# A decoder layer on one core: the middle layer on tokens sorted by matrix, in 14 pairs of tile and matrix

## Chip, cores and metric

The kernel runs on one core of a Trainium2 chip. The metric is the device time of one execution in microseconds (us).

## What is computed

The input x is 4 sequences of 256 tokens with 256 features, float32. Three layers follow each other, each added to its input and each working on the normalised input:

```python
x = x + attention(_layernorm(x), ...)          # 16 heads of 128, weights = codes * scales
x = x + xattn(_layernorm(x), tok, ctx, ctx, ctx)
x = x + moe(_layernorm(x), ...)                # 32 experts, 4 per token, and a shared one

# xattn, the middle layer: one of 4 matrices of 256 x 256 per token, by token id
expert_ids = jnp.minimum(tid // tokens_per_expert, E - 1)      # VOCAB 12500, E 4
for e in range(E):
    g = jax.nn.silu(jnp.einsum('bsd,fd->bsf', hidden_states, Wg[e]))
    u = jnp.einsum('bsd,fd->bsf', hidden_states, Wu[e])
    y = jnp.einsum('bsf,df->bsd', g * u, Wd[e])
    out = jnp.where((expert_ids == e)[..., None], y, out)
```

In this layer gate, up and down are the same matrix (ctx), so g = silu(z), u = z with one product z. In the last layer a token's 4 experts come from the router's scores, their outputs are weighted and summed.

## The kernel before

1024 tokens are 8 tiles of 128 (two halves of 4). Every float32 product of the first two layers is made of three float32r matmuls on high and low parts (mm3, L766 to L770). The operand on the moving side has 256 or 512 columns. Each engine has its own program and queue; they meet at semaphores. SyncE (SP) sends most DMAs, GpSimd (POOL) the indirect ones.

**Attention** runs in 8 groups of two heads; the last group (Plan.last) has four more slots to drain. Its last four output projection tiles are added to the residual x_acc by L1324, two token tiles at a time. The first half is normalised (ln_vector, ln_tensor, ln_high, ln_low, L689 to L759) beside this drain, the second behind it. GpSimd makes the weights' low parts (prep) and, in pieces of 128 tokens, the masks of the four matrices (masks, L606).

**Middle layer** (L892 to L934): 16 steps n of (half, matrix e, feature half ft). `pre` makes z of 512 tokens (6 matmuls of 512 columns), ScalarE takes the SiLU (L1220), GpSimd multiplies it with the mask (L656), VectorE with z (L1428), ScalarE and VectorE split it in high and low part (L1215, L1412), and `post`, three steps behind, adds four token tiles of 256 columns into the banks of the half (12 matmuls). All 8 steps of a half accumulate there, and L1418 adds them to x_acc. GpSimd also writes a piece of the table iota_s (L659) per step. The last half's normalisation goes on behind it (L1435), then router logits (L969), and the first expert weights (20 DMAs, L528 to L530) are sent by SyncE as soon as the last residual sum of attention is there (L519). Behind them in its queue stands the store of the normalised rows (L535), which the gathers read.

**Expert layer**: 64 tiles of 128 slots, in 8 trips of 8. GpSimd gathers the rows of the first 32 tiles (L667, a ring of 8). Per tile TensorE turns rows (L1056), runs gate and up (L942), turns the hidden part (L946) and runs down (L950); ScalarE takes SiLU and copies (L1235, L1240, L1292); VectorE copies and multiplies (L1555, L1561, L1442). SyncE stores each tile's output to memory (L550) and counts the stores that have landed. Trips 0 to 3 are unrolled with row work, 4 to 6 are a loop, 7 stands alone; on ScalarE and SyncE 1 to 6 and 1 to 7 are loops. VectorE does other work beside the tiles: slot tables in trips 0 to 2 (L1592 to L1623), the shared expert's sum in trip 3 (L1627), the weights of the four experts in trips 4 and 5 (L1566, L1572, L1579, L1586). From the table of slots GpSimd gathers the four outputs of every token, 32 gathers in all (L684), each after the stores that it needs; the first wait is for the table (S_NEED). When the tiles are done VectorE adds these (L1669), and SyncE stores the result.

## Time and profile before

| | us |
|---|---|
| median of 3 runs | 573.28 (571.64 to 573.55) |
| profiled execution | 574.22 |
| its span, first to last instruction | 572.3 |
| TensorE matmuls busy | 510.2 (89%) |
| VectorE, ScalarE, GpSimd busy | 424.0, 289.0, 201.8 |
| mean granted TensorE clock | 0.956 |

Times in rows are microseconds from the start of the span unless marked ns. PE is TensorE's matmuls, PEld its weight loads, DVE VectorE, ACT ScalarE, POOL GpSimd, SP SyncE. An arrow in brackets shows how long the engine had been idle and what released it. Matmuls are pipelined, so the distance of two starts tells more than the duration of one. PEclk is the granted clock as a share of the full one.

### The profile page before, as it was taken

What the parts mean: (1) busy time and instruction counts of PE and PEld (TensorE: products, weight loads), DVE (VectorE), ACT (ScalarE), POOL (GpSimd) and SP (SyncE); (2) the same over time, 40 slices, a digit from 0 to 9 for tenths busy, and PEclk for the clock granted to TensorE, in tenths of its full rate; (3) what the DMA queues carried; (4) which work ended last, traced back from release to release, by engine and by line L of the source; (5) the groups of instructions that cost most, each with busy time, mean ns of one, the idle gap of its engine ahead of it and who ended that gap; (6) DMA issues with size and microseconds to landing.
All of it is one profiled execution on the core that took longest, in us unless ns stands there. A gap on an engine that the chain in (4) does not pass through costs nothing.

```text
span 572.3 us, 11500 instructions
## 1 busy us (share of the span) xinstructions
PE 510.2 (89%) x3245; PEld 446.9 (78%) x3246; DVE 424.0 (74%) x1046; ACT 289.0 (50%) x794; POOL 201.8 (35%) x233
## 2 busy tenths in 40 slices
PE   7799999999999999999999979998877998796590
PEld 6688898998998988989989967897746886574380
DVE  6589988989889889898898787568846666341138
ACT  3566666656566566656565635444323443242250
POOL 3427604415215135053151005450074645606200
PEclk9999999999999999999999989998898999878596
DMA  7251212203102112011039409992023544424222
GB/s 195 89 145 55 65 30 56 64 1 80 39 27 64 27 37 64 18 55 37 0 105 354 167 0 289 302 292 74 1 83 117 160 146 131 128 93 130 73 92 101
DMA packets 59488, 57.10 MB, mean 100 GB/s; under 512 B 4080, under 2 KB 57152, under 8 KB 59328
## 3 DMA queue, kind: packets, MB, share of 16 engines
q1 hardware_dynamic: 56016, 48.16, 28.2%
q0 software_dynamic: 3168, 8.42, 5.3%
q8 instruction: 15, 0.25, 0.2%
q14 instruction: 17, 0.14, 0.1%
q10 hardware_dynamic: 272, 0.13, 0.1%
HBM read 46.21 MB, written 18.87 MB: 114 GB/s over the span
## 4 chain that ended last, share of the span: by engine, by line
PE 64%; DVE 18%; issue 10%; ACT 6%; POOL 1%; DVEq 1%; ACTq 0%; POOLq 0%
PE bank L768 12%; PE bank L769 12%; PE bank L770 12%; PE bank L942 12%; PE bank L950 6%; DVE rmax L1345 3%; DVE qk_lo L1337 3%; DVE nmax L1349 3%; PE bank L848 3%; ACT qk_hi L1145 2%; ACT prob L1153 2%; PE bank L946 2%; DVE pT_lo L1377 2%; PE bank L1056 2%; PE bank L774 1%
## 5 line engine op out<-in xcount | busy, mean ns | idle before, releaser
L1153 ACT ACTIVATE prob<-bank,nmax 128x256 f32<-128x256 f32 x128 | 59.5, 470 | 108.7 <-DVE nmax L1349 108.7
L585 POOL TENSOR_TENSOR w_lo<-st_c,w_hi 128x512 fp32r<-128x512 f32 x32 | 41.3, 1291 | 193.2 <-ACT w_hi L1116 193.2
L942 PE MATMUL bank<-moe_w,xT 128*128 x256 | 72.0, 407 | 3.7 <-DVE xT L1561 3.6
L1442 DVE TENSOR_TENSOR hid<-bank,sg 128x128 f32<-128x128 f32 x64 | 18.6, 291 | 59.0 <-ACT sg L1235 27.3
L1337 DVE SCALAR_TENSOR_TENSOR qk_lo<-bank,b_col,qk_hi 128x512 fp32r<-128x512 f32 x64 | 47.9, 748 | 16.1 <-ACT qk_hi L1145 15.3
L942 PEld LDWEIGHTS bank<-moe_w,xT 128*128 128x128 f32 x256 | 49.3, 204 | 12.2 <-issue 6.0
L768 PE MATMUL bank<-hT_hi,w_lo 128*128 128x512 f32 x128 | 52.8, 413 | 5.5 <-DVE qk_lo L1337 2.9
L1345 DVE TENSOR_REDUCE rmax<-bank 128x2 f32<-128x512 f32 x64 | 43.9, 686 | 13.8 <-PE bank L770 13.7
L769 PE MATMUL bank<-hT_lo,w_hi 128*128 128x512 f32 x128 | 50.7, 396 | 0.0
L770 PE MATMUL bank<-hT_hi,w_hi 128*128 128x512 f32 x128 | 50.4, 394 | 0.0
L667 POOL DMA_INDIRECT x_in<-h_dram,source x32 | 32.1, 1004 | 48.2 <-DVE source L1525 28.5
L1235 ACT ACTIVATE sg<-bank 128x128 f32<-128x128 f32 x64 | 17.8, 279 | 61.8 <-PE bank L942 47.5
L1145 ACT ACTIVATE qk_hi<-bank,b_col 128x512 fp32r<-128x512 f32 x64 | 44.0, 687 | 7.8 <-PE bank L770 6.2
L1369 DVE TENSOR_SCALAR prob<-prob,rinv 128x256 f32<-128x256 f32 x128 | 46.0, 401 | 2.3
L1377 DVE TENSOR_TENSOR pT_lo<-bank,pT_hi 128x512 fp32r<-128x512 f32 x64 | 43.6, 681 | 1.7 <-ACT pT_hi L1179 1.7
L582 POOL TENSOR_TENSOR st_c<-st_c,st_s 128x512 f32<-128x512 f32 x32 | 41.1, 1285 | 10.5 <-DVE h_row L727 5.6
L768 PE MATMUL bank<-pT_hi,v_lo 128*128 128x256 f32 x128 | 42.0, 328 | 2.7 <-DVE pT_lo L1377 2.7
L950 PE MATMUL bank<-moe_w,hidT 128*128 x128 | 41.9, 412 | 2.6 <-ACT hidT L1240 2.4
L684 POOL DMA_INDIRECT yg<-y_dram,y_slot x32 | 31.4, 982 | 34.9 <-SPq L544 26.9
L848 PE MATMUL bank<-ident,prob 128*128 128x128 f32 x256 | 38.9, 275 | 0.2
L768 PE MATMUL bank<-w_hi,oT_lo 128*128 128x256 f32 x128 | 36.8, 288 | 2.4 <-DVE qk_lo L1337 2.4
L1179 ACT CAST pT_hi<-bank 128x512 fp32r<-128x512 f32 x64 | 38.1, 595 | 0.6 <-PE bank L848 0.6
(213 smaller groups left out, 1558.9 us busy)
## 6 DMA issues: line engine op xcount, KB each, us to landing
y_dram<-ysb SPq DMA_DIRECT2D x64, 128.0 KB
moe_w<-in_w_gate SPq DMA_DIRECT2D x8, 512.0 KB, 8.4
moe_w<-in_w_up SPq DMA_DIRECT2D x8, 512.0 KB, 7.7
moe_w<-in_w_down SPq DMA_DIRECT2D x4, 1024.0 KB, 8.5
st_c<-in_wq_codes SPq DMA_DIRECT2D x16, 128.0 KB
st_c<-in_wk_codes SPq DMA_DIRECT2D x16, 128.0 KB
st_c<-in_wv_codes SPq DMA_DIRECT2D x8, 256.0 KB
st_c<-in_wo_codes SPq DMA_DIRECT2D x8, 256.0 KB
```

The source lines that it names most:

```text
L768: pe.matmul(o, l_lo, r_hi, start=start, stop=False, skip_group_check=share)
L769: pe.matmul(o, l_hi, r_lo, start=False, stop=False, skip_group_check=share)
L770: return pe.matmul(o, l_hi, r_hi, start=False, stop=stop, skip_group_check=share)
L848: mm = pe.transpose(bP[i % 2][:, kt * S + qt * P:kt * S + qt * P + P], prob[:, i % 4, qt, kt * P:kt * P + P], ident[:, :])
L942: mm = pe.matmul(o, xT_of(kt), w, start=kt == 0, stop=kt == KT - 1)
L950: pe.matmul(bY[n % 2][:, 0:D], hidT[:, n % 2, :], w, start=True, stop=True).then_inc(t_dn, 1)
L1145: act.activation(qk_hi[:, hp, m, n * HALF:(n + 1) * HALF], src[:, :], ACT.Identity, bias=b_col[:, bass.ds(g_h + m * H, 1)]).then_inc(a_qk, 1)
L1153: ex = act.activation(prob[:, i % 4, qt, :], bS[i % 2][:, qt * S:(qt + 1) * S], ACT.Exp, bias=nmax[:, i % 2, qt:qt + 1], scale=SCALE, accu ...
L1337: dve.scalar_tensor_tensor(out=qk_lo[:, hp, m, n * HALF:(n + 1) * HALF], in0=src[:, :], scalar=b_col[:, bass.ds(g_h + m * H, 1)], in1=qk_h ...
L1345: dve.tensor_reduce(rmax[:, i % 2, :], bS[i % 2][:, :].rearrange("p (q k) -> p q k", q=2), AX.X, ALU.max).then_inc(v_m1, 1)
L1369: sc = dve.tensor_scalar(prob[:, j % 4, qt, :], prob[:, j % 4, qt, :], rinv[:, j % 2, qt:qt + 1], None, ALU.mult)
L1377: dve.tensor_tensor(pT_lo[:, j % 2, :, :].rearrange("p a b -> p (a b)"), bP[j % 2][:, :], pT_hi[:, j % 2, :, :].rearrange("p a b -> p (a b ...
```

## The change

Tokens of each half are sorted by matrix. Their places are worked out early: the token ids are loaded one per partition (a DMA of 4-byte elements instead of a broadcast), GpSimd compares them in the first group (kinds), TensorE counts them with eight small bf16 matmuls in the last group (token_ranks), and GpSimd makes destinations (places) and the list of segments (segments): a segment is a pair of a sorted tile and a matrix, and with 4 tiles and 4 matrices there are at most 7 per half. The masks of the attention groups go away.

When the last sums of attention are there, GpSimd scatters each token tile to memory in sorted order, and SyncE loads the tiles back (8 + 8 DMAs). Both normalisations of the middle layer follow that. TensorE runs 14 and 8 extra matmuls (keep_warm) around the first half's transposes. Then come 14 pairs: ScalarE copies the tile's high and low parts to a fixed place (segment_copy, address from a register), `pre` makes z with tokens on partitions (6 matmuls of 256 columns against the pair's matrix), ScalarE the SiLU, VectorE one operation for product and mask, TensorE two transposes (`mid`), then high and low part, `post` (6 matmuls of 256 columns) and a sum into the x_acc tile given by a register. In the second half's and the last layer's normalisations the root is a power on GpSimd, and the rows of the last layer's first half are scaled by GpSimd (ln_pool). The expert weights' loads wait for the reload of the second half and for the segments.

All rows stay in sorted order until the end. Token order returns beside the expert tiles: SyncE stores a table of slots and weights (trip 2) and the residual (trip 3), GpSimd gathers eight tiles of each by destination (the table between the last eight row gathers), and ordering the slots moves from trip 1 to trip 4, finding what each gather needs from trip 2 to trip 4 (TABLE_TRIP). The expert weights' products move from trips 4 and 5 into trip 1, the shared sum from trip 3 to 2. Trip 4 is unrolled on TensorE and VectorE, trips 0 to 3 on SyncE.

```diff
 VOCAB = 12500
 HALF = 512
 NH = T // HALF
-MASK_STEPS = 2 * 4 - 2
+HT = NT // NH
+SEGS = T // NH // P + NROUTE - 1
+WAIT_ROWS, WAIT_COPY = 14, 8
+NSEG = NH * SEGS
 NE, TOPK, FI = 32, 4, 128
...
+            for half in range(NH):
+                sp.wait_ge(d_xs[half], 16 * HT)
+                for t in range(half * HT, (half + 1) * HT):
+                    sp.dma_start(x_acc[:, t, :], xs_dram.rearrange("(t p) d -> t p d", p=P)[t]).then_inc(d_xa[t], 16)
+
             sp.wait_ge(v_w, 4 * G + 1)
+            sp.wait_ge(p_seg, 1)
             EB = NE // 4
             for q in range(4):
...
                 first = isinstance(it, int) and it == 0
                 for u in range(STEPS):
+                    if isinstance(it, int) and it == 2 and u == 0:
+                        sp.wait_ge(v_slot, S_TAB)
+                        sp.dma_start(tab_dram.rearrange("(t p) k -> p t k", p=P), tab[:, :, :]).then_inc(d_tab, 16)
+                    if isinstance(it, int) and it == 3 and u == 4:
+                        sp.wait_ge(v_sh, NT)
+                        sp.dma_start(x2_dram.rearrange("(t p) d -> p t d", p=P), x_acc[:, :, :]).then_inc(d_x2, 16)
...
+            def scatter(half):
+
+                pool.wait_ge(p_dest, 1)
+                for t in range(half * HT, (half + 1) * HT):
+                    if t % 2 == 0:
+                        pool.wait_ge(v_w, Plan(G - 1).w_done_count(t // 2, True))
+                    pool.indirect_dma_start(out=xs_dram, out_offset=bass.IndirectOffsetOnAxis(ap=dest[:, t:t + 1], axis=0),
+                                            in_=x_acc[:, t, :], in_offset=None).then_inc(d_xs[half], 16)
 
             def constants():
...
                     if pl.first and c == WC:
                         constants()
-                if not pl.last:
-                    masks(g)
+                        kinds()
...
+            for half in range(NH):
+                scatter(half)
+            ln_root(pool, 1, 1)
+            for n in range(PIECES):
+                wait(pool, t_z, min(n + 1, NSEG))
+                some = SLOTS // PIECES
                 pool.iota(iota_s[:, n * some:(n + 1) * some, :], pattern=[[1, some], [0, CH]], base=n * some, channel_multiplier=0,
                           allow_small_or_imprecise_dtypes=True).then_inc(p_many, 1)
+                if n == SEGS + 1:
+                    ln_pool(pool, 2, 0)
...
-
+                t = n - (ROWS - NT)
+                if t >= 0:
+                    pool.wait_ge(d_tab, 16)
+                    pool.indirect_dma_start(out=tab_t[:, t, :], out_offset=None, in_=tab_dram,
+                                            in_offset=bass.IndirectOffsetOnAxis(ap=dest[:, t:t + 1], axis=0)).then_inc(d_tabs, 16)
+
+            pool.wait_ge(d_x2, 16)
+            for t in range(NT):
+                pool.indirect_dma_start(out=x_acc[:, t, :], out_offset=None, in_=x2_dram,
+                                        in_offset=bass.IndirectOffsetOnAxis(ap=dest[:, t:t + 1], axis=0)).then_inc(d_xt, 16)
 
             at = [pool.alloc_register(f"need{i}") for i in range(2)]
...
+            def token_ranks():
+
...
+                rank = bO[0][:, S:S + n].rearrange("p (g t) -> p g t", t=HT)
+                pe.matmul(bO[0][:, S:S + n], before[:, :], of_kind[:, :, :].rearrange("p e t -> p (e t)"), start=True, stop=False,
+                          skip_group_check=True)
...
+            def keep_warm(n):
+
+                for i in range(n):
+                    pe.matmul(Z_AT[0][:, :], cT_hi[:, 0, 0, 0:P], cT_hi[:, 0, :, :].rearrange("p k d -> p (k d)"), start=True, stop=True)
+
...
             def pre(n):
 
-                half, e, ft = routed(n)
-                wait(pe, v_t, n - 3)
+                pe.wait_ge(a_copy, n + 1)
+                wait(pe, v_t, n - 1)
                 for kt in range(KT):
-                    mm = mm3(Z_BANKS[n % 4][:, :], cT_hi[:, e, kt, ft * P:ft * P + P], cT_lo[:, e, kt, ft * P:ft * P + P],
-                             hT_hi[:, kt, half * HALF:(half + 1) * HALF], hT_lo[:, kt, half * HALF:(half + 1) * HALF],
-                             kt == 0, kt == KT - 1)
+                    mm = mm3(Z_AT[n % 2][:, 0:D], h_seg[:, n % 2, kt * P:kt * P + P], h_seg[:, n % 2, (KT + kt) * P:(KT + kt) * P + P],
+                             kind_part(cT_hi, n, kt), kind_part(cT_lo, n, kt), kt == 0, kt == KT - 1)
                 mm.then_inc(t_z, 1)
 
+            def mid(n):
+
+                pe.wait_ge(v_t, n + 1)
+                wait(pe, v_g, n - 1)
+                for kt in range(KT):
+                    mm = pe.transpose(TURN_AT[n % 2][:, kt * P:kt * P + P], gm[:, n % 2, kt * P:kt * P + P], ident[:, :])
+                mm.then_inc(t_turn, 1)
+
             def post(n):
 
-                half, e, ft = routed(n)
                 pe.wait_ge(v_g, n + 1)
-                for j in range(4):
-                    yb = ENDS[half][j // 2][:, (j % 2) * D:(j % 2) * D + D]
-                    mm = mm3(yb, gu_hi[:, n % 2, j * P:(j + 1) * P], gu_lo[:, n % 2, j * P:(j + 1) * P],
-                             cT_hi[:, e, ft, :], cT_lo[:, e, ft, :], False, e == NROUTE - 1 and ft == KT - 1, True)
+                wait(pe, v_y, n - 1)
+                for kt in range(KT):
+                    mm = mm3(y_at(n), gu_hi[:, n % 2, kt * P:kt * P + P], gu_lo[:, n % 2, kt * P:kt * P + P],
+                             kind_part(cT_hi, n, kt), kind_part(cT_lo, n, kt), kt == 0, kt == KT - 1)
                 mm.then_inc(t_y, 1)
 
...
+            keep_warm(WAIT_ROWS)
+            ln_tensor(pe, 1, 0, ENDS[0])
+            keep_warm(WAIT_COPY)
             pe.wait_ge(v_c, NROUTE)
-            for n in range(RSTEPS + BEHIND):
-                if n % (RSTEPS // 2) == 0 and n < RSTEPS:
-                    pe.wait_ge(v_lnlo, 6 if n == 0 else 8)
-                if n == 3:
+            for n in range(NSEG + 2):
...
+            def segment_copy(n):
+
+                at = act.snap(tile_at_reg[word(n) % STEPS], min_val=0, max_val=(NT - 1) * 2 * KT * P)
+                act.wait_ge(v_lnlo, 6 + 2 * half_of(n))
+                act.wait_ge(a_ln, 6 + 2 * half_of(n))
+                wait(act, t_z, n - 1)
+                apart(act)
+                act.copy(h_seg[:, n % 2, :], hT_tiles[:, :, :, :, :].rearrange("p t l k s -> p (t l k s)")[:, bass.ds(at, 2 * KT * P)]).then_inc(a_copy, 1)
+
+            def routed_silu(n):
...
+            def routed_product(n):
+
+                dve.wait_ge(a_z, n + 1)
+                wait(dve, t_turn, n - 1)
+                dve.scalar_tensor_tensor(out=gm[:, n % 2, :], in0=gact[:, n % 2, :],
+                                         scalar=seg_mask[:, half_of(n), n % SEGS:n % SEGS + 1],
+                                         in1=Z_AT[n % 2][:, 0:D], op0=ALU.mult, op1=ALU.mult).then_inc(v_t, 1)
+
+            def routed_low(n):
+
+                dve.wait_ge(a_g, n + 1)
+                wait(dve, t_y, n - 1)
+                dve.tensor_tensor(gu_lo[:, n % 2, :], TURN_AT[n % 2][:, 0:D], gu_hi[:, n % 2, :], ALU.subtract).then_inc(v_g, 1)
+
+            def routed_sum(n):
+
+                row = dve.snap(at[word(n) % STEPS], min_val=0, max_val=(NT - 1) * D)
+                dve.wait_ge(t_y, n + 1)
+                wait(dve, v_y, n)
+                here = x_acc[:, :, :].rearrange("p t d -> p (t d)")[:, bass.ds(row, D)]
+                apart(dve)
+                dve.tensor_tensor(here, y_at(n), here, ALU.add).then_inc(v_y, 1)
+
+            norm = {(n, half): ln_vector(dve, n, half, x_acc) for n, half in LN_KINDS[2:]}
...
             pairs = [(half, slice(k, k + 2)) for half in range(2) for k in (0, 2)]
             trip(0, STEPS, False, {u: (lambda u=u: (extra_sum if u % 2 else extra_work)(*pairs[u // 2]),) for u in range(STEPS)})
-            trip(1, STEPS, False, {0: (slots,), **{1 + u: (lambda u=u: order(2 * u),) for u in range(4)}, 5: (slots_ordered,)})
-            trip(LAST_TRIP, STEPS, False, {}, {1: last_slots, 3: tiles_needed})
-            trip(ROW_TRIPS - 1, STEPS - 1, False, {u: (lambda u=u: add_shared(u),) for u in range(NT)})
-            trip(ROW_TRIPS, 0, False, {0: (lambda: gain_work(0),), 2: (lambda: gain_sum(0),), 4: (lambda: gain_work(1),),
-                                       6: (lambda: gain_sum(1),)})
-            trip(ROW_TRIPS + 1, 0, False, {0: (gain_scale,), 2: (gain_order,)})
-            with dve.Fori(ROW_TRIPS + 2, TRIPS - 1) as it:
+            trip(1, STEPS, False, {0: (lambda: gain_work(0),), 1: (lambda: gain_sum(0),), 2: (lambda: gain_work(1),),
+                                   3: (lambda: gain_sum(1),), 4: (gain_scale,), 5: (slots,)})
+            trip(2, STEPS, False, {u: (lambda u=u: add_shared(u),) for u in range(NT)})
+            trip(ROW_TRIPS - 1, STEPS - 1, False, {})
+            trip(TABLE_TRIP, 0, False, {0: (table_back, lambda: order(0), lambda: order(2)),
+                                        1: (lambda: order(4), lambda: order(6), slots_ordered),
+                                        3: (last_slots,), 5: (tiles_needed,), 6: (gain_order,)})
+            with dve.Fori(TABLE_TRIP + 1, TRIPS - 1) as it:
                 trip(it, 0, False, {})
...
```

## Rows read from the trace of the kernel before

**Rows 1.** Busy time by stage (stretch, length, then each engine, clock, DMA share, GB/s)
```profile
342.00:392.00 50.00, 48.16 (x304) 41.72 (x304) 33.15 (x74) 22.89 (x39) 24.00 (x32) 1.00 0.95 253
392.00:423.50 31.50, 25.48 (x162) 19.89 (x160) 23.86 (x99) 11.79 (x33) 6.19 (x6) 0.89 0.17 55
423.50:484.00 60.50, 56.27 (x292) 45.71 (x292) 40.16 (x130) 24.95 (x93) 31.97 (x33) 0.97 0.45 135
484.00:557.00 73.00, 53.56 (x213) 40.70 (x213) 20.44 (x72) 25.44 (x95) 25.40 (x26) 0.81 0.33 104
```

**Rows 2.** Timeline of TensorE at the middle layer's ends (start, duration, operation)
```profile
342.14 0.47 PE L768 MATMUL bank<-hT_hi,cT_lo 128*128 128x512 f32 x1
...
391.71 0.28 PE L770 MATMUL bank<-cT_hi,pT_hi 128*128 128x256 f32 x1
391.83 1.03 PE L747 MATMUL bank<-ident,h_row 128*128 128x128 f32 x8
...
397.27 1.17 PE L747 MATMUL bank<-ident,h_row 128*128 128x128 f32 x4
```

**Rows 3.** Timeline of GpSimd, two masking steps of the middle layer
```profile
382.82 1.17 POOL L656 TENSOR_TENSOR x_in<-x_in,mask 128x512 f32<-128x512 f32 x1 [1.30 <-ACT x_in L1220]
...
385.61 1.17 POOL L656 TENSOR_TENSOR x_in<-x_in,mask 128x512 f32<-128x512 f32 x1 [1.30 <-ACT x_in L1220]
```

**Rows 4.** Timeline of TensorE, then VectorE, at the end of attention
```profile
330.57 0.58 PE L768 MATMUL bank<-pT_hi,v_lo 128*128 128x256 f32 x1 [1.77 <-DVE pT_lo L1377]
330.95 0.42 PE L769 MATMUL bank<-pT_lo,v_hi 128*128 128x256 f32 x1
...
338.75 1.74 PE L747 MATMUL bank<-ident,h_row 128*128 128x128 f32 x8 [1.04 <-DVE h_row L727]
...
330.82 0.68 DVE L1324 TENSOR_TENSOR x_acc<-bank,x_acc 128x512 f32<-128x512 f32 x1
...
340.70 1.29 DVE L759 TENSOR_TENSOR hT_lo<-bank,hT_hi 128x512 fp32r<-128x512 f32 x2 [0.44 <-ACT hT_hi L753]
341.95 0.69 DVE L1324 TENSOR_TENSOR x_acc<-bank,x_acc 128x512 f32<-128x512 f32 x1
342.68 1.40 DVE L698 BATCH_NORM_STATS2 bn<-x_acc 128x6 f32<-128x256 f32 x4
...
345.84 1.38 DVE L727 TENSOR_SCALAR h_row<-x_acc,mv,rstd 128x256 f32<-128x256 f32 x4
```

**Rows 5.** Groups by line (busy, mean ns), then DMAs (KB, us to landing)
```profile
L1384 DVE SCALAR_TENSOR_TENSOR oT_lo<-bank,b_col,oT_hi 128x256 fp32r<-128x256 f32 x11 | 5.2, 477 | 0.8 <-ACT oT_hi L1188 0.8
L1292 ACT COPY ysb<-bank 128x256 f32<-128x256 f32 x64 | 23.9, 373 | 17.3 <-PE bank L950 8.3 <-remote 3.1 <-issue 1.2
L1215 ACT CAST pT_hi<-prob 128x512 fp32r<-128x512 f32 x16 | 9.9, 620 | 13.6 <-PE bank L770 10.2 <-DVE prob L1428 3.5
L667 POOL DMA_INDIRECT x_in<-h_dram,source x32 | 32.1, 1004 | 48.2 <-DVE source L1525 28.5 <-issue 14.3 <-PE bank L1056 3.5
L612 POOL TENSOR_SCALAR mask<-ids 128x128 bf16<-128x128 int32 x32 | 17.4, 544 | 2.6
...
h_dram<-h_row SPq DMA_DIRECT2D x2, 512.0 KB, 3.0
out<-x_acc SPq DMA_DIRECT2D x4, 256.0 KB, 2.1
```

**Rows 6.** Busy time with and without bursts of gathers (columns as in rows 1)
```profile
480.00:486.20 6.20, 3.83 (x19) 2.97 (x18) 2.27 (x7) 1.49 (x6) 4.93 (x5) 1.00 0.58 163
...
489.00:501.00 12.00, 9.08 (x36) 6.46 (x35) 4.45 (x11) 3.01 (x11) 9.33 (x9) 0.92 0.47 137
501.00:516.50 15.50, 14.39 (x58) 11.31 (x58) 6.39 (x26) 7.44 (x28) 0.96 (x2) 0.78 0.28 93
516.50:534.00 17.50, 7.21 (x31) 4.96 (x29) 1.67 (x6) 2.58 (x10) 13.27 (x14) 0.75 0.43 128
```

**Rows 7.** Expert layer: one stop of TensorE (timeline), one group by line
```profile
534.88 0.48 PE L946 MATMUL bank<-ident,hid 128*128 128x128 f32 x1 [8.72 <-issue]
...
L1566 DVE TENSOR_TENSOR work<-hot,score 128x512 f32<-128x512 f16 x2 | 2.1, 1061 | 0.0
```

More of the change, by code:

```diff
@@ L554, in store @@
                         stored(u - AFTER + STEPS, it - 1)
-            store(0)
-            with sp.Fori(1, TRIPS) as it:
+            for it in range(ROW_TRIPS):
+                store(it)
+            with sp.Fori(ROW_TRIPS, TRIPS) as it:
                 store(it)
@@ L888, in _, with load_kinds @@
             over_groups(pe, body)
-            def zero(half):
-                for yb in ENDS[half]:
-                    pe.matmul(yb[:, :], zeros[:, :], zeros[:, 0:1].to_broadcast([1, HALF]), start=True, stop=True)
+            at = [pe.alloc_register(f"at{i}") for i in range(STEPS)]
+            def load_kinds(w):
+                apart(pe)
+                pe.reg_load(at[w % 2 * PACK:w % 2 * PACK + PACK],
+                            seg_expert[0:1, :, :].rearrange("p h i -> p (h i)")[:, w * PACK:(w + 1) * PACK])
@@ new lines, in body, with load_segments @@
+                    if pl.last and i == 4:
+                        dve.wait_ge(p_bounds, 1)
+                        for half in range(NH):
+                            ins = dve.max(sorted_b[:, half, :], bounds[:, half, :])
+                        ins.then_inc(v_sorted, 1)
+            over_groups(dve, body)
+            at = [dve.alloc_register(f"row{i}") for i in range(STEPS)]
+            def load_segments(w):
+                apart(dve)
+                dve.reg_load(at[w % 2 * PACK:w % 2 * PACK + PACK],
+                             seg_row[0:1, :, :].rearrange("p h i -> p (h i)")[:, w * PACK:(w + 1) * PACK])
@@ L1437, in _ @@
+            for part in norm[2, 1][1:]:
                 part()
@@ L1544, in _ @@
             own(dve.memset(xT_all[:, :, ROWS * SLOTS:(ROWS + 1) * SLOTS], 0.0))
-            at = [dve.alloc_register(f"row{i}") for i in range(STEPS)]
             def load_rows(word, first):
@@ L1627, in add_shared, with trip @@
                 dve.tensor_tensor(x_acc[:, t, :], shared[:, t, :], x_acc[:, t, :], ALU.add).then_inc(v_sh, 1)
-            def trip(it, rows, last, beside, between={}):
+            def trip(it, rows, last, beside):
                 for u in range(STEPS):
```

443 lines of the change are left out of this document (310 added, 133 removed).

## Prediction

> **What bounds the kernel now.** I read the busy time by stage first [rows 1]. The reader should see that the time lies in three kinds of stretch. From 342 to 392 us, the middle layer, TensorE is busy 48.2 of 50 us at full clock: this stage is bound by the number of matmuls. From 392 to 423.5 it is 25.5 of 31.5: short chains over all engines (normalisation, routing tables). From 484 to 557 it is only 53.6 of 73 at a granted clock of 0.81: the expert loop stands still for some 28 us. Then I took the times of the first and last matmul of the middle stage [rows 2], its step [rows 3], the end of attention [rows 4], prices of single operations [rows 5], and the expert loop in the stretches in which GpSimd sends gathers and those in which it doesn't [rows 6]. The profiled execution took 574.2 us (span 572.3 and 1.9 around it), 0.9 above the median of 573.3; I make the sum against it and take 0.9 off.
>
> **Middle layer.** Before, every token goes through all four matrices: 16 steps (half, matrix, half of the features) of 6 matmuls of 512 columns and 12 of 256. A step takes 2.79 us, from one masking on GpSimd to the next, 382.82 to 385.61 [rows 3]; 256-column matmuls follow each other at 0.12 us (391.71 to 391.83) [rows 2]. The stage runs from 342.1 to 391.9 [rows 2], 49.8 us. After, 512 tokens sorted by matrix need at most 7 pairs of a tile and a matrix, 14 in both halves, each 12 matmuls of 256 columns and two transposes: 12 x 0.12 + 0.25 = 1.7 us on TensorE, where 0.25 is twice the 0.12 pitch, by the nearest row. Does another engine set the pace? VectorE has three operations of 256 columns (product with mask, low part, sum into the residual): the nearest row is 0.48 [rows 5], pipelined 0.40, so 1.2 to 1.45. ScalarE has a copy of 512 (0.62), SiLU and high part of 256 (0.37 each) [rows 5]: 1.36. Both are below 1.7, but near it. The masking on GpSimd, 1.17 [rows 3], and its hop leave the chain. So 13 x 1.7 = 22.1; the last pair has nothing to overlap with, and its way is matmuls 0.7, SiLU 0.4, product 0.45, transposes 0.35, high 0.4, low 0.45, matmuls 0.7 and six hops near 0.07: 3.9. Two normalisation blocks of eight transposes (1.03 us at 391.83 [rows 2], 0.9 to the next matmul) lie in the stage: 1.8. VectorE also gets the statistics, the row scaling and the low parts of the second half, 1.4 + 0.6 + 0.8 + 1.4 + 1.3 us, in pairs 0 to 5; its slack of 0.4 a pair doesn't hold all of it: 1.5, my choice between 0 and 4. Sum 22.1 + 3.9 + 1.8 + 1.5 = 29.3, a gain of 20.5.
>
> **The gap before it.** Before, the first middle matmul starts right behind attention, since the first half was normalised beside the drain. Now token tiles are scattered to memory in sorted order and loaded again. The gating chain is half 0: its last residual sum starts at 330.82 and ends at 331.5 [rows 4]; two scatters at the pitch of an indirect DMA, 1.0 and 0.3 of issue [rows 5]: 334.1; landing 2.1 to 3.0 us by the two stores to memory [rows 5], I take 2.5: 336.6; four loads 0.35 each plus 2.1: 340.1. Statistics' start to row scaling's start is 3.2 us (342.68 to 345.84 [rows 4]), but three of the four tiles are done before the last lands, so 2.2: 342.3; from the first transposes to the low part's end 3.2 (338.75 to 341.99 [rows 4]) plus 0.5 until a row is there: 346.0; the new ScalarE copy 0.6: 346.6. The eight small rank matmuls in the last trip of attention are bounded by 0 and 8 x 0.12 = 1.0; I take 0.5, by the middle. The first pair thus starts at 347.1 instead of 342.1: a loss of 5.0 (3 to 9: the two landings were measured for large transfers and may be 2 us shorter together, or 4 longer if they queue behind each other). Evictions aren't late next: half 0 no longer takes VectorE's time in the drain, so the last sum, now 341.95 in program order behind 340.70 [rows 4], comes near 339. About 20 small GpSimd operations (segments) run from 322.7; the nearest row, 0.54 for 128 columns [rows 5], bounds them at 11 us, and nearer to 5 since they have under 100 elements; they end between 328 and 334, and beyond 331.5 each us delays the scatter. The 22 extra matmuls (14 + 8 of 512 columns, 5 us) lie wholly in this gap. What they protect against is seen at 330.57: after 1.77 us idle a 256-column matmul takes 0.58 and the next 0.41 instead of 0.28 [rows 4]. With them about 1 us of clock loss remains in the range; without them I would add 2.
>
> The stores to memory here land after 2.1 and 3.0 us [rows 5], though SyncE sends them and not GpSimd. The Trainium skill, *DMA: Bandwidth & Descriptors*, Anatomy of one DMA, gives GpSimd's transfers about 2.0 us fixed, mostly the receipt of the write, longest to memory; by that the scatter would land 0.5 us sooner, and no row here shows a scatter's landing.
>
> **SyncE's queue.** The expert weights (20 loads, 36 us of issuing) now wait for the reload of half 1 and start near 347 instead of 342.7; they end issuing near 384 and land by 393. Behind them is queued the store of the normalised rows, 10 us later than it could be; its reader, the first row gather, comes near 399. No cost; from 15 us of delay on it would cost.
>
> **After the middle.** The last half's statistics are taken tile by tile, the root comes from GpSimd and no second 512-column sum stands ahead of them. First transposes of that half come at 397.27, 5.5 us after the last matmul [rows 2]; now 0.4 + 0.35 + 0.55 + 0.5 (root, between 0.1 and 1) + 0.8 + 0.5 = 3.1, but the chain through VectorE's routing gains only its own 1.9. Routing tables are unchanged. So far +5.0 - 20.5 - 1.9 = -17.4.
>
> **Expert stage.** Two products of 1.06 us (and two sums of about the same) move from the fifth trip into the second [rows 7], where VectorE's tile of 1.63 us is full (copy 0.56, copy 0.21, beside-work 0.42, product 0.4): 4 x 0.6 = +2.5. Eight gathers of table rows, eight of x, two stores and a fifth unrolled trip are new. The price is not in their bytes. While GpSimd sends gathers back to back, the loop nearly stops: 480 to 486.2 and 516.5 to 534 TensorE is busy 3.8 of 6.2 and 7.2 of 17.5 us; between them, 501 to 516.5 with one gather, 14.4 of 15.5 [rows 6]. The longest stop, 8.7 us, ends at 534.88, half a us after the last gather was sent [rows 7]. So 35 us of bursts cost 28: 0.8 per us of burst. Eight x gathers add 10.4 us of burst (+8 at this price), table gathers 10.4 (they lie beside row gathers, whose 1.3 us each leaves gaps of 0.3 in the 1.63 step, and these cost nothing there). Against this the slot gathers come later (the table is ready near tile 37 instead of 19), can't run past the tile they read, and more of them fall beyond the loop's need. I take +5, between 0 and +21. Combining at the end is unchanged. Total -17.4 + 2.5 + 5 = -9.9: 574.2 - 9.9 - 0.9 = 563.4.
>
> **Rivals.** (1) The stops belong to the loop's turns, not to gathers; one turn goes, none is added, extra gathers are hidden: -17.4 + 2.5 = -14.9, 558.4. For it: the stops lie in the looped trips; against it: the turn from the fifth to sixth looped trip, within 501 to 516.5, shows none, and the stops are not at multiples of 8 tiles. 0.25. This is the rule of the Trainium skill, *Runtime: NRT & Kernel Launch*, Instruction fetch mechanics: a taken branch to code outside a small window fetches it by DMA first. (2) The pairs are bound by hops and by VectorE and ScalarE, which are within 0.3 us of TensorE: 2.1 us a pair, 13 x 0.4 = 5.2: 568.6. For it: three engines touch a pair seven times; against: two pairs are always in flight. 0.19. (3) Slower: in the expert stage every added or displaced gather costs the full 0.8. Eight x, eight table gathers (20.8 us) and the four that lay alone at 472 to 480 (5 us) in one chain with the rest: 25.8 x 0.8 = 20.6 in place of 5: +5.7, 578.1. It decides from 14.9 us of added stops on. 0.14. That the change doesn't do what it says would show as middle matmuls of 512 columns; the code excludes it.
>
> **Chances.** Forecast 0.42, rivals 0.25, 0.19, 0.14. The forecast's own range is 559 to 568; for 8 in 10 I go from 554 (clean, short landings) to 575 (slow pairs with dear gathers), which leaves rival 3 and small tails out. A difference of 0.3%, 1.7 us, is what can be told from none. Faster: 0.41 + 0.25 + 0.16 = 0.82; within 0.05; slower 0.13.
>
> **What will show it.** First pair's matmul at 345 to 349; pairs 1.65 to 1.8 us apart; last near 376; first expert matmul near 406 instead of 423.6; then the time from there to the combination: 133.4 before, 141 forecast, 136 by rival 1, 156 by rival 3. I am wrong if the sorted tiles come back later than 342, if the pair's pace is over 2 us, or if GpSimd's chain of gathers ends after the experts.

## The result: slower, by 3.1%

The changed kernel took 591.1 us in the median of four runs (586.8 to 594.5), the kernel before 573.4 beside it: a ratio of 1.031, 95% interval 1.024 to 1.038. The profiled execution took 586.8 (span 585.0), 12.5 more than that of before. It is the shortest of the four: what follows explains those 12.5 us, of the 17.7 between the medians.

The page of the changed kernel: busy time of each engine, the granted clock in 40 slices, the chain that ended last, the group of gate and up products.

```profile
PE 501.6 (86%) x3179; PEld 436.6 (75%) x3180; DVE 413.4 (71%) x1046; ACT 286.0 (49%) x800; POOL 198.1 (34%) x239
...
PEclk9999999999999999999999999979799679759696
...
PE 62%; DVE 15%; issue 13%; ACT 4%; POOL 3%; DMA 1%; DVEq 1%; SPq 0%; ACTq 0%; POOLq 0%
...
L1183 PE MATMUL bank<-moe_w,xT 128*128 x256 | 77.2, 430 | 9.3 <-DVE xT L1873 5.2
```

TensorE works 8.6 us less than before and the kernel is longer: what was taken out of the middle came back as standing time in the last third, where the clock row has its gaps. (Below, an x gather fetches the rows of an expert tile, a y gather expert outputs for the tokens, a table gather the slots and weights of the tokens, and the gathers of the sums bring the residual back to token order.) Busy time by stage (columns as in [rows 1]: stretch, length, each engine, clock, DMA share, GB/s), middle layer first, the rest the expert loop:

```profile
345.60:377.30 31.70, 29.07 (x229) 26.92 (x230) 25.19 (x79) 19.53 (x47) 13.26 (x27) 1.00 1.07 288
...
423.00:452.00 29.00, 28.90 (x149) 22.54 (x148) 23.81 (x68) 13.23 (x48) 13.34 (x15) 1.00 0.44 128
452.00:477.00 25.00, 14.14 (x47) 9.62 (x45) 5.96 (x18) 4.51 (x16) 11.54 (x12) 0.66 0.22 60
477.00:491.50 14.50, 14.32 (x74) 11.50 (x73) 7.77 (x34) 6.87 (x26) 3.84 (x4) 1.00 0.56 179
491.50:527.60 36.10, 18.34 (x57) 13.10 (x56) 5.44 (x22) 6.84 (x25) 20.80 (x23) 0.67 0.39 115
```

Where [rows 1] has the middle layer at 48.2 busy of 50 us, it is now 29.1 of 31.7. But 452 to 477, whose tiles (22 to 25) had no stop before, holds 14 us of TensorE's work in 25, and 491.5 to 527.6 holds 18 in 36. The granted clock of these two stretches is 0.66 and 0.67, so matmuls right behind a stop are slower too; the losses counted below include that. TensorE and GpSimd at the middle's ends and at the start of the experts (start, duration, operation; in brackets the idle time before and its releaser):

```profile
345.60 0.38 PE L963 MATMUL bank<-cT_hi,pT_lo 128*128 x1 [0.75 <-ACT pT_lo L1464]
...
375.30 0.28 PE L965 MATMUL bank<-cT_hi,pT_hi 128*128 x1
...
406.86 1.13 PE L1183 MATMUL bank<-moe_w,xT 128*128 x4 [1.03 <-DVE xT L1873]
...
398.92 1.18 POOL L838 DMA_INDIRECT x_in<-h_dram,source  x1 [20.64 <-DVE source L1839]
```

The first matmul of the experts comes at 406.9; it was 423.6. The 16.7 us are there. From it to the combination (VectorE's adding of the four outputs per token, from 569.7) are 162.8 us; before they were 133.4. These 29.4 are the result.

**What a stop looks like.** GpSimd sends 15 y gathers without a pause from 499.7 to 518.1, and one more at 518.8. In the middle of them, TensorE and then ScalarE; the last two lines are TensorE and VectorE at the end of the earlier run of table and x gathers (447.9 to 466.9):

```profile
506.92 0.33 PE L1187 MATMUL bank<-ident,hid 128*128 128x128 f32 x1 [0.91 <-DVE hid L1756]
508.82 0.69 PE L1191 MATMUL bank<-moe_w,hidT 128*128 x2 [1.57 <-issue]
509.67 1.97 PE L1183 MATMUL bank<-moe_w,xT 128*128 x4 [0.16 <-issue]
521.57 0.48 PE L1187 MATMUL bank<-ident,hid 128*128 128x128 f32 x1 [9.92 <-issue]
...
508.31 0.27 ACT L1512 COPY hidT<-bank 128x128 f32<-128x128 f32 x1 [1.86 <-PE bank L1187]
511.87 0.37 ACT L1563 COPY ysb<-bank 128x256 f32<-128x256 f32 x1 [3.29 <-remote]
520.91 0.28 ACT L1507 ACTIVATE sg<-bank 128x128 f32<-128x128 f32 x1 [8.67 <-remote]
...
467.15 0.63 PE L1295 MATMUL bank<-ident,x_in 128*128 128x128 f32 x2
469.29 0.42 DVE L1867 COPY xT_all<-bank 128x256 f32<-128x256 f32 x1 [5.06 <-PE bank L1295]
```

Each ScalarE operation starts long after the matmul it waits for: 1.06 us behind 507.25, 2.4 behind 509.51, and the activation 9.3 us behind the products that by the profile ended at 511.64. In the other direction nothing is late: the transpose at 521.57 follows VectorE's product, which follows the activation at 520.91. VectorE is late behind TensorE as well: its copy at 469.29 starts 1.5 us behind the transposes that ended at 467.78. In e9 (below), where nothing stops, neither engine starts more than 0.23 us behind TensorE from 440 us on, where the profile names TensorE as what it waited for. What comes late is thus what TensorE reports as done (its semaphore update). Since the profile models the ends of matmuls, it can't tell a late report from matmuls that really end late.

**Where the 29.4 us are.** Transposes of the hidden rows (L1187, one a tile) start 1.63 us apart in the first 30 tiles and 1.41 after, where nothing holds them up (their pace). Time over that pace: tiles 1 to 4 6.7 us (before 6.0), tiles 22 to 26 16.9 (before 0), tiles 36 to 43 24.9 (before, 32 to 34 and 36 to 40: 13.5 in all), tiles 49 to 52 14.6 (before 16.9). Together 63.1 instead of 36.4; tiles 9 to 13 take 2.2 us more than their pace, and that leaves half a us.

### The profile page after: what moved, and what is told of

It reads as the page before. It is cut to its first block, busy times and chain, and to the rows that moved or that the text cites. A ratio compares the mean times of both kernels' runs of the same rounds, so it can differ in the third digit from the quotient of the medians.

```text
span 585.0 us, 11594 instructions
## 1 busy us (share of the span) xinstructions
PE 501.6 (86%) x3179; PEld 436.6 (75%) x3180; DVE 413.4 (71%) x1046; ACT 286.0 (49%) x800; POOL 198.1 (34%) x239
## 4 chain that ended last, share of the span: by engine, by line
PE 62%; DVE 15%; issue 13%; ACT 4%; POOL 3%; DMA 1%; DVEq 1%; SPq 0%; ACTq 0%; POOLq 0%
PE bank L963 12%; PE bank L1183 12%; PE bank L965 11%; PE bank L964 11%; PE bank L1191 5%; PE bank L1043 3%; DVE qk_lo L1608 3%; DVE rmax L1616 2%; PE bank L1187 2%; DVE nmax L1620 2%; ACT prob L1393 1%; PE bank L1295 1%; ACT qk_hi L1385 1%; PE bank L969 1%; DVE x_acc L1986 1%
## 5 line engine op out<-in xcount | busy, mean ns | idle before, releaser
L1183 PE MATMUL bank<-moe_w,xT 128*128 x256 | 77.2, 430 | 9.3 <-DVE xT L1873 5.2
L1183 PEld LDWEIGHTS bank<-moe_w,xT 128*128 128x128 f32 x256 | 52.1, 216 | 19.5 <-issue 11.9
L1191 PE MATMUL bank<-moe_w,hidT 128*128 x128 | 44.9, 437 | 5.5 <-ACT hidT L1512 3.0
L1187 PE MATMUL bank<-ident,hid 128*128 128x128 f32 x64 | 19.8, 309 | 28.3 <-issue 25.0
```

What stands on the lines that cost most here:

```text
L1183: mm = pe.matmul(o, xT_of(kt), w, start=kt == 0, stop=kt == KT - 1)
L1191: pe.matmul(bY[n % 2][:, 0:D], hidT[:, n % 2, :], w, start=True, stop=True).then_inc(t_dn, 1)
```

## The experiments

Theory A: a run of gathers that GpSimd issues back to back (every 1.25 to 1.30 us) holds up TensorE's reports, the semaphore updates that other engines wait for. Rivals: B, each gather costs its price wherever it lies; C, the stops belong to the turns of the loops.

**e1, the y gathers of before one a tile.**

```diff
                 pool.wait_ge(y_done, ...)
+                pool.wait_ge(t_gu, SH + TILES // 2 + n)
                 pool.indirect_dma_start(out=home(k)[:, t, :], ...
```

> The kernel before, with one more wait ahead of each of the 32 late row gathers (L684): gather n isn't issued until TensorE has done the first product of expert tile 32 + n, so that one gather falls on each tile (1.41 us apart instead of 1.25, and never a backlog). Nothing is left out. Theory A (a run of gathers issued back to back is what stops the expert tiles, by holding up what TensorE reports): the stops at tiles 32-33, 37-40 and 49-52 of before (about 5.3 + 8 + 17 = 30 us over the 1.41 pace) go, and the time falls to 543-552 us. Theory B (each gather costs its 0.8 us per us of issue wherever it lies, or the bytes do): the same 32 gathers, so 570-575. Theory C (the stops belong to the turns of the loops over trips and the gathers only meet them): 570-575 too.

Measured: 550.1 us against 573.0, ratio 0.960 (0.955 to 0.965). The stretch in which the 32 gathers now lie (columns as above):

```profile
480.00:531.00 51.00, 49.99 (x228) 38.05 (x227) 22.60 (x76) 25.52 (x98) 30.44 (x32) 1.00 0.56 160
```

Same gathers, same loops, TensorE busy 50 of 51 us: B and C fall. Only the first burst is left: tiles 1 to 3 take 10.4 us there, 5.6 over their pace.

**e2, eight gathers more in one run.**

```diff
+            for t in range(NT):
+                pool.indirect_dma_start(out=home(0)[:, t, :], in_=h_dram, ... source[:, t:t + 1] ...)
             pool.wait_ge(v_slot, S_NEED)
```

> The kernel before, with 8 gathers of 128 rows of 1 KB added in one unbroken run, between the last of its 32 x gathers and the first of its 32 y gathers; their rows are overwritten later by the y gathers, so the result is the same. Theory A (back-to-back issue stops the tiles): 8 gathers are 10 us of issue, of which the first 4 us cost nothing, so +5 to +8 us: 578-581. Theory B (price per us of issue, 0.8): +8, 581. Theory C (turns of loops): nothing, 573.

Measured: 583.2 against 573.0, ratio 1.018 (1.013 to 1.023). The added run and what follows it (columns as above):

```profile
465.30:481.00 15.70, 10.34 (x42) 7.49 (x41) 5.68 (x17) 3.72 (x14) 9.73 (x10) 0.73 0.41 127
```

Tiles 24 to 26, at pace before, lose 9.4 us. A run of 10.4 us costs about its length, and not 0.8 of it less a free start; this size A, and B with it, had missed by 2 us. C, which expected no change, falls here too.

**e3, no return to token order; e4, the return kept, its gathers spread.** In e3 the table and the sums are used as they are (five edits), so that its output rows stay in sorted order: that part of the computation is left out. In e4:

```diff
-                t = n - (ROWS - NT)              # table gather beside x gather n
+            for t in range(NT):                  # table gathers behind the x gathers
+                    pool.wait_ge(t_gu, SH + ROWS - NT + t - 1)
...
+                pool.wait_ge(t_gu, SH + ROWS + t)                  # sums
...
+                pool.wait_ge(t_gu, SH + ROWS + NT + n * 3 // 4)    # y
```

> The changed kernel without the return to token order: no table store, no 8 table gathers, no store of the sums and no 8 gathers of them; the slots and gains of the sorted tokens are used as they are, so the rows come out in sorted order (that part of the computation is left out). If the loss is the 16 added gathers alone (theories A and B): the expert stage falls back to before's 131-133 us and the forecast's 17 us gain ahead of it stands, 555-559 us. If it is something else in the changed expert stage (the moved gain products, the unrolled trips, the shifted phase of tiles and gathers): over 570.

> The changed kernel with its late gathers spread: the 8 table gathers follow the 32 x gathers, one a tile from tile 24, the 8 gathers of the sums one a tile from tile 32, and the 32 y gathers three in four tiles... four in three tiles from tile 40. Nothing is left out. Theory A: the stops in tiles 22-25 and 36-43 go (about 17 + 25 us) and those of the y gathers shrink: 540-560 us. Theory B (price per gather): unchanged, 585-592, and C the same.

Measured: e3 565.5, ratio 0.986 (0.981 to 0.991); e4 552.3, ratio 0.961 (0.956 to 0.967). e3 missed its range by 6.5 us: its first hidden transpose came at 412.4, 3.4 us later than in the changed kernel, and its y gathers, 14 of them in one run, cost tiles 41 to 44 and 49 to 51 32.9 us over pace where those of before cost 30.4. But without the 16 gathers the changed kernel is the faster one. In e4 no gather is missing and 39 us of the 591 are gone: more than the loss goes with the spacing of the gathers alone. But the spacing isn't all. e4 (552.3) isn't below e1 (550.1), though its first tile comes 13.1 us earlier: its 64 tiles take 124.3 us from first to last, those of e1 106.1. Its 40 gathers of sums and outputs (columns as above):

```profile
474.00:536.00 62.00, 49.37 (x216) 35.38 (x214) 17.77 (x74) 23.71 (x93) 38.29 (x40) 1.00 0.52 151
```

They go out in groups of up to 5 less than 0.6 us apart, those of e1 in groups of up to 3, and TensorE stands for 12.6 of 62 us, against 1 of 51 in e1. Whether it is these groups or the 16 added gathers themselves that cost the 18 us, these two runs don't tell.

**Four more kernels, and a kernel before of 539 us.** Every ratio here compares kernels that ran together on one chip, the kernel before among them. The next four:

> A version meant to beat both. From the changed kernel: the tokens stay in sorted order to the end, so the table store, the 8 table gathers, the store and the 8 gathers of the sums are gone; instead the token numbers (4 bytes a row) are scattered by the same destinations beside the middle layer's pairs, one a pair, read back once, and the 8 output tiles are scattered by them as their combination ends. The x gathers are held to one a tile from the start (gather n waits for tile n - 3) and the y gathers to one a tile from tile 32. Nothing is left out. Theory A: e3_no_return (565.5) less its three stops of y gathers (tiles 41-44 and 49-51, about 18 + 14 us beyond pace) and some 6 us of the first burst, plus 1 to 2 us for scattering the last output: 527-537 us. Rival (a gather costs whatever its spacing): 560-566.

> The kernel before with the y gathers one a tile (as e1_before_paced, 550.1 us) and now the first 11 x gathers held too: gather n waits for TensorE's tile n - 3. Nothing is left out. Theory A: the 7 us that tiles 1 to 4 lose at the end of the first run of 11 gathers in e1 go too: 541-546 us. Rival (that first loss is a start-up cost of the expert stage, not of the gathers): 550.

> e2_before_plus8 (583.2 us, 10 us of back-to-back gathers added ahead of the y gathers) with the 8 added gathers replaced by 20 additions of 128 x 256 on GpSimd itself in the same place, 10 to 20 us of work and no transfer. If the stops come from GpSimd being busy without a pause (its share of a memory port, say), +8 or more as in e2: over 580. If they come from the issue of indirect transfers (theory A): 571-575, as before.

> e2_before_plus8 with the 8 added gathers cut to 64 rows each (half the rows, half the bytes, the same number of gather instructions). If the stops grow with the rows moved: the run keeps half the load, stops begin later or not at all, 573-576. If they go by GpSimd's time in gathers and a gather of 64 rows takes as long as one of 128: 581-584 as e2. If the issue time itself halves to about 0.5 us the run is 6.4 us long and the loss 2-4 us.

Measured, beside a kernel before that now took 539.2 us and not 573, on another chip: e5 550.5 (ratio 1.019, 1.017 to 1.022), e6 544.0 (1.009, 1.007 to 1.012), e7 540.7 (1.002, 1.001 to 1.003), e8 538.9 (1.000, 0.998 to 1.001). Nothing stops here: e7 sends its 32 y gathers in one run of 41 us and its 64 tiles take 97.6 us, where those of before took 131.5. So these four don't test theory A, and their expectations, made for a session like the first (I call the kernels that ran together a session), say nothing for or against it. Two things they do tell. Holding the x gathers to the tiles costs 5 us where there are no stops to save (e6). And e5 shows a price that I had not on the list. GpSimd in e5, the last y gather and the first two of the eight scatters of the output:

```profile
521.88 1.21 POOL L861 DMA_INDIRECT yg<-y_dram,y_slot  x1 [0.30 <-issue]
523.40 9.27 POOL L866 DMA_INDIRECT out<-x_acc,home_row  x1 [0.31 <-DVE x_acc L1986]
532.98 0.98 POOL L866 DMA_INDIRECT out<-x_acc,home_row  x1 [0.30 <-issue]
```

The scatter that was to lie beside VectorE's combination (519.0 to 531.8) takes 9.27 us and ends 0.9 us after it; then each takes 0.98. So all eight end behind the combination, and they cost more than the version had saved.

**The change in a session without stops, and three more kernels.** From here on the expectations speak of chips that stop and chips that don't, as I took it to be; what is known is only that a session is of one kind or the other, as its kernel before shows (below, under what is open). e9 is the changed kernel itself; e10 and e11 are e1 with, between x and y gathers, 12 additions of 128 x 256 on GpSimd, or 8 gathers of 64 rows (`out=home(0)[0:64, t, :]`); e12 is e3 with the y gathers spread.

> The changed kernel once more, with nothing edited, because the chip now counts: the kernel before took 573 us on one chip and 539 us on another, where its runs of gathers 1.25 us apart (34 in a row) stopped no tile. On a chip that stops (before 573): 587-594 as first measured. On one that doesn't (before 539): the 17 us gained ahead of the expert stage stand, less 2 to 5 us for the DVE work that lies over the row trips and for tiles that wait for gathered data: 522-528.

> e1_before_paced (y gathers one a tile) with 12 additions of 128 x 256 on GpSimd, 0.83 us each and 10 us in one unbroken run, between the x and the y gathers, where the tiles run quietly. On a chip that stops: if GpSimd's being busy without a pause stops the tiles, +8 over e1's 550.1, so 558; if only gathers do, 550 with tiles 24 to 30 at their pace of 1.63 us. On a chip that doesn't stop: e1 and this within 1 us of each other either way.

> e1_before_paced with a run of 8 gathers of 64 rows each in the same place; one of them takes GpSimd 0.95 us like one of 128 rows (measured in e8_half_rows, on the chip without stops), so the run is as long and holds half the rows. On a chip that stops: if the number of gather instructions and their closeness count, tiles 24 to 26 lose 9.4 us as in e2_before_plus8 (559); if the rows moved count, 0 to 4 us (550-554). On the other kind of chip: no loss.

> e3_no_return (the changed kernel without the return to token order, so its rows come out sorted: that part is left out) with its 32 y gathers spread evenly over tiles 38 to 63. On a chip that stops: e3's 565.5 less the 33 us that its tiles 41-44 and 49-51 lost over their pace, so 532-538, which is the forecast's gain of 15-17 us ahead of the experts against e1_before_paced (550.1). On a chip that doesn't: 522-526.

It was again a session without stops. (The 34 gathers in a row of e9's expectation stand in no profile; e7 and e8 show 32.) Measured: before 539.2; e9 533.3, ratio 0.986 (0.981 to 0.992); e10 539.6 (1.001) and e11 539.2 (1.000), which tell nothing here; e12, whose output is in sorted order like e3's, 525.9, 0.974 (0.972 to 0.977), inside its range. The same change is thus 1.4% (5.9 us) faster where TensorE isn't held up; 9.9 us had been forecast. The tiles of e9 beside its interleaved table and x gathers, and beside 36 of a run of 40 gathers 1.25 us apart:

```profile
442.00:460.00 18.00, 16.08 (x87) 12.74 (x86) 10.92 (x33) 7.31 (x28) 13.74 (x15) 1.00 0.43 119
...
466.00:511.00 45.00, 44.82 (x219) 36.37 (x218) 19.58 (x74) 24.81 (x94) 34.10 (x36) 1.00 0.66 192
```

TensorE is busy 44.8 of 45 us beside it. e9 still misses its expectation by 5 us, and its trace says where. Tiles 26 to 29 take 10.1 us instead of 6.5: the table gathers stand between the x gathers, so x rows come every 2.6 us and a tile needs one every 1.63. And its y gathers end after the experts (last hidden transpose at 511.41; GpSimd, then VectorE):

```profile
514.12 1.28 POOL L864 DMA_INDIRECT yg<-y_dram,y_slot  x1 [0.30 <-issue]
515.70 8.01 POOL L864 DMA_INDIRECT yg<-y_dram,y_slot  x1 [0.30 <-issue]
...
511.27 11.62 DVE L1986 SCALAR_TENSOR_TENSOR x_acc<-yg,factor,x_acc 128x256 f32<-128x256 f32 x29
525.57 1.28 DVE L1986 SCALAR_TENSOR_TENSOR x_acc<-yg,factor,x_acc 128x256 f32<-128x256 f32 x3 [2.68 <-DMA yg<-y_dram,y_slot]
```

The last gather takes 8.01 us and ends 0.8 us after the 29 combinations, and the last three of these wait for it: from the last tile to the end are 20.1 us, in e10 15.2. Against e10: 16.2 us earlier at the first tile, 5.4 lost in the tiles, 4.9 behind them; 5.9 us are left, the difference of their spans.

**e13 to e15: a more even layout, and what of a gather counts.** e13 is e4 with the table gathers over tiles 23 to 29, the sums stored half a trip earlier and gathered from tile 29 on, and the y gathers at `SH + ROWS + 5 + n * 26 // 31`; e14 and e15 are e10 and e11 again.

> e4_after_paced with its gathers laid out more evenly, nothing left out: the 8 table gathers over tiles 23 to 29 right behind the x gathers, the store of the sums half a trip earlier and their 8 gathers from tile 29 on, one a tile, and the 32 y gathers 26 to 31 tiles (tiles 37 to 63) instead of 24. On a chip that stops: e4's 552.3 less 3 to 8 us, as its places with two gathers close together, each of which cost about 1.5 us over pace, get fewer and lie further apart: 544-549. On one that doesn't: the changed kernel's 533.3 less 3.7 us (its tiles 26 to 29 waited for x rows whose gathers stood between table gathers) and less some 4 of the 5 us by which its y gathers ran on behind the last tile: 525-529.

> e10_adds_paced again, for a chip that stops: 12 additions on GpSimd without a pause (10 us) beside tiles 24 to 30. Only the gathers stop the tiles: 550, as e1_before_paced. GpSimd's being busy does: 558. (A chip that doesn't stop gives 539-540 as before and tells nothing.)

> e11_half_rows_paced again, for a chip that stops: 8 gathers of 64 rows without a pause. Instructions and their closeness count: about 559, as tiles 24 to 26 lost 9.4 us in e2_before_plus8. Rows count: 550-554. (A chip that doesn't stop gives 539-540 and tells nothing.)

A session with stops (before 573.4). Measured: e13 549.6, ratio 0.960 (0.956 to 0.963); e14 548.5, 0.959 (0.955 to 0.962); e15 558.7, 0.978 (0.973 to 0.982). e13 missed its range (544 to 549) by 0.6 us, and e14 (the kernel before with its y gathers held, and 10 us of additions) is no slower than it: e13's first tile comes 12.6 us earlier, but its 64 tiles take 124.0 us and those of e14 107.0. The more even layout didn't remove the 17 to 18 us that e4 had left. The added load in e14, then in e15 (columns as above):

```profile
466.00:476.00 10.00, 10.00 (x56) 8.42 (x56) 8.60 (x23) 4.94 (x19) 8.57 (x13) 1.00 0.32 104
```

```profile
466.00:482.50 16.50, 9.80 (x40) 7.13 (x39) 5.44 (x17) 3.44 (x13) 7.64 (x9) 0.79 0.26 75
```

GpSimd busy without a pause for 9.2 us costs TensorE nothing; eight gathers of half the rows cost tiles 24 to 26 9.4 us, to the tenth what eight whole ones cost in e2. So it is the gather instructions, and neither GpSimd's being busy nor the number of rows and bytes.

**e16 to e18.** e16 is e1 with e2's eight gathers and an addition of 128 x 32 behind each, e17 is e6 and e18 is e13.

> e1_before_paced with 8 added gathers of 128 rows between the x and the y gathers, as in e2_before_plus8, but with an addition of 128 x 32 on GpSimd behind each, so that the gathers are some 1.45 to 1.6 us apart instead of 1.25 though GpSimd never pauses. On a chip that stops (before 573): if the closeness of the gathers is what counts, tiles 24 to 26 keep their pace, 549-552; if their number is, the 9.4 us of e2 are lost, 559. On one that doesn't (539): 539-541 either way.

> e6_before_paced_all again, for a chip that stops: the first 11 x gathers too wait for tile n - 3, with the y gathers one a tile. The 7 us that tiles 1 to 3 lose there in e1 (550.1) are the gathers' and go, while the waiting itself costs the 5 us seen on the chip without stops (544.0 against 539.2): 547-550. If they are a start-up cost of the stage: 555.

> e13_after_spread again (549.6 on a chip that stops), for a chip that doesn't: the changed kernel's 533.3 there less 3.7 us of late x rows and less 4 of the 5 us behind the last tile, 525-529. On a chip that stops it gives 549-550 again.

A session without stops (before 539.0): e16 538.8, ratio 0.999 (0.998 to 1.001), e17 543.8, 1.008 (1.006 to 1.010), neither of which tells anything new; e18 526.8, ratio 0.979 (0.976 to 0.982), as expected. With e13 this is a version that beats both kernels in both kinds of session: 549.6 where they take 573 and 591, 526.8 where they take 539 and 533. It is the change itself with its gathers laid out. But where there are stops, what beats both is the spacing: there it isn't faster than the kernel before with its y gathers held (e1 550.1, e14 548.5). Without stops it is, by 12.8 us (e10 539.6, in another session; the kernel before took 539.2 and 539.0 beside them).

**Open.** What keeps e4 and e13 at 124 us from first to last tile in the sessions with stops: e18, the same kernel as e13, takes 98.8 without them. Two sessions had stops (before at 573.0 and 573.4, like the measurement of the result at 573.4), three had none (539.2, 539.2, 539.0), and within a session nearly all runs of a kernel lie within 1.3% of each other. Program and input are the same. I first took it for a trait of the chip, but one chip number stands for a session of each kind (the numbers may repeat between machines), so whether it is the chip, its surroundings or its condition at the time isn't known, and no row names it. Open is too whether the rate or the missing pause makes a run harmful; the kernel for it (e16) met a session without stops. And whether the loss at tiles 1 to 4 (6.7 us) is that of the first 11 gathers: its time says so, but e6 and e17 ran where it doesn't occur. And by what way gathers and TensorE's reports are linked.

## Why the prediction was wrong

**Ahead of the experts it held.** First pair at 345.6 (347.1 forecast, 345 to 349 allowed); end of the last middle matmul 375.6 (376); so the middle took 30.0 us, 29.3 forecast; first expert matmul 406.9 (406). Gain 16.7 us for a forecast of 17.4. That the sum is so close is in part luck: the gap before cost 1.5 us less than forecast, and behind the middle layer, where 1.9 us were to be gained, it was 0.3 (last middle matmul to first expert matmul 31.3 us, before 31.6). In the six other profiles of versions with this middle layer (e5 aside), the first expert matmul came between 407.1 and 410.3. The pairs came 1.6 to 2.2 us apart at first, 2.7 and 2.8 around the second half's normalisation and 1.6 to 1.9 later (three of their transposes at 360.81, 362.44 and 364.07), so rival 2, which wanted 2.1 for all, falls. The gap before the middle layer was 3.5 us, not 5.0: the statistics of the reloaded tiles began at 337.7, right behind the last residual sum (337.1), so the way through memory was over before VectorE was free. The fourth scatter was issued at 331.91 and the first load of SyncE, which waits for all four, at 334.36: 2.45 us, the 2.5 of the forecast. The 2.0 us that the prediction cites from the Trainium skill, *DMA: Bandwidth & Descriptors*, Anatomy of one DMA, are the fixed part of a transfer alone, to which that page adds a part for the bytes; this scatter took longer than 2.0.

**The moved gain products held**: +2.2 us over tiles 9 to 13 for +2.5 forecast.

**The added gathers were the failed step**: +5, between 0 and +21, where the tiles over pace and the rest gave +27. Two parts of the cost were wrong, and a credit was worth nothing.

1. "Table gathers ... lie beside row gathers, whose 1.3 us each leaves gaps of 0.3 in the 1.63 step, and these cost nothing there." 1.25 + 1.30 is 2.55 us and doesn't fit into a step of 1.63. So the pair of them made one unbroken run of 15, 447.9 to 466.9, in place of spaced gathers, and that run cost 16.9 us (tiles 22 to 26). In e9, without stops, the same step costs 3.6 us, since x rows come too slowly.
2. The price of 0.8 us per us of burst was an average over stretches of 6 to 17.5 us, and I took it as the worst case. (Its 28 us for 35 can't be read from [rows 6], where TensorE stands for 15.6 of 35.7 us; counted by tiles it is 30.4 us over pace for 39 us of y gathers, again 0.8.) e2 and e15 measured 0.9 to 1.0 for a run of 10 us that stands alone. Before's short ones (two gathers at 472, one at 503.8) had cost nothing. In the changed kernel they are gone: the eight of the sums and the first 16 y gathers stand almost in one, 486.8 to 519.7, and tiles 36 to 43 lost 24.9 us.
3. The credit that I gave, slot gathers that "fall beyond the loop's need", was nothing here: the last y gather of the changed kernel ended at 550.6, 19 us before the last tile (569.8). In e9, where the tiles aren't held up, they do run beyond the loop, and that is a cost of 4.9 us, just the condition under which I said I would be wrong.

**The rivals.** (Rival 3's time should read 579.0: 573.3 + 5.7. The 578.1 takes the 0.9 us off twice.) Rival 1 (loop turns, and with it the Trainium skill's rule in *Runtime: NRT & Kernel Launch*, Instruction fetch mechanics, as the cause of these stops) falls with e1: the turns are all there and the stops aren't. The trace agrees with that page nowhere as to these stops. Rival 3 had the right sign and the right place, at 0.14; its 156 us from first expert matmul to combination were 162.8. Its mechanism was half right: gathers in one chain with the rest do stop the loop, but a fixed price for every added gather is not what e1 shows, where 32 of them cost TensorE 1 us of 51. It is what the profile bore out better than I weighed it: [rows 6] showed that bursts stop the loop, and the change lengthened the bursts. I had counted gathers, and should have drawn up GpSimd's issue order with its times, burst by burst.

## What to carry to other kernels

Before adding work to a queue whose bursts already stand beside stops, lay out that queue's issue times: what counts is how long a run without a gap gets, not its share of the time. Tie each gather to a consumer's tile: one wait a gather took 23 us (4.0%) off the kernel before and 39 us off the changed one, where there were stops. And measure a change that lives by a hundred small hand-overs in more than one session, with the kernel before beside it; here its sign depended on it. Compare a repaired version with an equally repaired kernel before: beside e1 and e14 the 39 us are no gain of the change.

## What the runs showed of the hardware that I hadn't expected

- The same kernel took 573 us in two sessions of the experiments and 539 in three. Spans of the profiled runs with and without stops differ by about as much as the experts' tiles do: before 572.3, with 131.5 us from its first to its last tile; e7, which differs from it only in additions ahead of its y gathers, 539.2 and 97.6.
- A gather of 64 rows takes GpSimd 0.94 to 0.96 us, like one of 128.
- Of the gathers and scatters that began beside VectorE's combination the first three ran at 0.95 to 1.28 us and the fourth not until VectorE had stopped: 9.27 us (e5), 8.01 (e9), each until 0.8 to 0.9 us after VectorE's last operation before a pause. The Trainium skill, *SBUF — State Buffer*, Who interferes with whom, says that a VectorE instruction with two inputs from SBUF contends with a GpSimd instruction that reads SBUF; these combinations have two such inputs and the transfers read their row numbers there. The trace agrees for the fourth and not for the three before it. The same section says that TensorE and ScalarE never wait on anyone; in the sessions with stops TensorE's reports were up to 9.3 us late beside gathers by the modelled ends of its matmuls, and no run here tells by what way.
